# Full attention on one core: in the first head, two relu-lifted key differences per query tile and seven score banks in place of one difference and three banks

## What is computed

```python
q = (h @ wq).reshape(B, S, N_HEADS, D_HEAD)
k = (h @ wk).reshape(B, S, N_HEADS, D_HEAD)
v = (h @ wv).reshape(B, S, N_HEADS, D_HEAD)
scores = jnp.einsum('bshd,bthd->bhst', q, k) * scale
attn = jax.nn.softmax(scores, axis=-1)
ctx = jnp.einsum('bhst,bthd->bshd', attn, v).reshape(B, S, d)
X = X + ctx @ wo
```

## Time and profile before

| what | value |
|---|---|
| median of 3 runs | 2500.25 us (2498.46 to 2501.71) |
| the profiled execution: its time, its span | 2503.76 us, 2502.0 us |
| PE busy, 15464 matmuls | 2108.6 us, 84% |
| DVE busy, 4863 instructions | 1808.9 us, 72% |
| ACT busy, 2370 instructions | 1621.5 us, 65% |
| L1371 DVE maxima, 1520 | 963.6 us, mean 683 ns |
| L1368 DVE add and maximum, 264 | 182.0 us, mean 689 ns |
| L1297 ACT lifts, 264 | 157.6 us, mean 597 ns |

### The profile page before, as it was taken

The page is one execution under the profiler, slowest core; times in us unless marked ns, Lnnn a source line. Parts: engine busy times, 40 slices in busy tenths (PEclk is TensorE's granted clock), DMA queues, the critical chain, the costliest instruction groups (busy, mean ns, idle before and its releaser), DMA issues. The chain is left out here.

```text
span 2502.0 us, 44024 instructions
## 1 busy us (share of the span) xinstructions
PE 2108.6 (84%) x15464; PEld 914.0 (37%) x15464; DVE 1808.9 (72%) x4863; ACT 1621.5 (65%) x2370; POOL 516.0 (21%) x797
## 2 busy tenths in 40 slices
PE   6487488869377799999999987948999999999696
PEld 2365145657245222222222236721222222222375
DVE  7733695443585889999999925368999999996443
ACT  3033355334345479999999973424999999999443
POOL 6165131147111000000000014720000000000075
PEclk9589599879689689999999998965999999999798
DMA  2312560221480511111111021115011011010213
GB/s 67 95 44 75 76 118 16 71 57 50 85 146 16 147 25 22 24 31 23 23 30 24 8 75 32 52 38 155 16 30 30 16 30 30 16 30 2 74 47 87
DMA packets 94697, 127.17 MB, mean 51 GB/s; under 512 B 20906, under 2 KB 72592, under 8 KB 94480
## 3 DMA queue, kind: packets, MB, share of 16 engines
q1 hardware_dynamic: 82832, 102.99, 18.8%
q0 software_dynamic: 11648, 21.36, 2.9%
HBM read 79.88 MB, written 42.40 MB: 49 GB/s over the span
## 5 line engine op out<-in xcount | busy, mean ns | idle before, releaser
L1371 DVE TENSOR_REDUCE pair_mx<-ps 128x1 f32<-128x512 f32 x1520 | 963.6, 683 | 78.4 <-PE ps L1175 72.8
L1323 ACT ACTIVATE prob<-ps 128x1024 f32<-128x1024 f32 x1024 | 990.1, 1025 | 41.9 <-PE ps L1206 20.7
L1175 PE MATMUL ps<-k_stack,q_stack 48*128 48x512 bf16 x2048 | 592.9, 402 | 29.3 <-PEq L928 9.0
L1220 PE MATMUL ps<-prob,v_head 128*32 128x512 f32 x4096 | 547.7, 607 | 1.5 <-ACT prob L1323 1.0
L1206 PE MATMUL ps<-q_stack,k_stack 51*128 51x512 bf16 x2048 | 447.9, 384 | 6.0 <-ACT prob L1323 3.7
L1175 PEld LDWEIGHTS ps<-k_stack,q_stack 48*128 48x128 bf16 x2048 | 153.1, 94 | 497.5 <-DVE pair_mx L1371 354.3
L2252 DVE TENSOR_TENSOR hid<-silu,ps 128x256 f32<-128x256 f32 (+1 forms) x190 | 87.8, 463 | 246.9 <-PE ps L2105 166.2
L1206 PEld LDWEIGHTS ps<-q_stack,k_stack 51*128 51x128 bf16 x2048 | 105.1, 94 | 299.3 <-ACT prob L1323 266.8
L1722 DVE CUSTOM_DVE_ANT_0 ps<-ps,mask 128x256 f32<-128x256 f32 (+2 forms) x512 | 179.7, 418 | 40.4 <-PE ps L1526 38.2
L1297 ACT ACTIVATE qk<-ps 128x512 f32<-128x512 f32 x264 | 157.6, 597 | 62.6 <-PE ps L1175 56.0
L2105 PE MATMUL ps<-weight_raw,block 128*128 x632 | 193.9, 430 | 0.0
(11 more groups left out here) (249 smaller groups left out, 2293.1 us busy)
## 6 DMA issues: line engine op xcount, KB each, us to landing
q_stack<-image_dram SPq DMA_DIRECT2D x88, 192.0 KB, 4.6
k_stack<-k_wide_dram SPq DMA_DIRECT2D x60, 240.0 KB, 5.4
arena<-e_rows SPq DMA_DIRECT2D x32, 256.0 KB, 4.7
k_stack<-image_dram SPq DMA_DIRECT2D x32, 192.0 KB, 4.4
image_dram<-parts SPq DMA_DIRECT2D x28, 192.0 KB, 5.2
k_wide_dram<-parts SPq DMA_DIRECT2D x2, 1800.0 KB, 17.2
image_dram<-parts SPq DMA_DIRECT2D x28, 128.0 KB, 5.0
weight_raw<-in_L_ffn_Wg_dram SPq DMA_DIRECT2D x6, 528.0 KB, 4.7
```

Source lines behind the costliest of these rows:

```text
L1175: nc.tensor.matmul(max_bank(n), rows_of(c.q_stack, b, g, ROWS, slice(t * P, (t + 1) * P)), rows_of(c.k_rows, b, g, ROWS, slice(k * CHUNK, ...
L1220: ins = nc.tensor.matmul(out, c.v_head[:, e % 2, kb, :], unit, start=(kb == 0), stop=(kb == TILES - 1), skip_group_check=True)
L1323: nc.scalar.activation(c.prob[:, u % P_UNITS, :], c.ps[:, 2 * (u % 2) * CHUNK:2 * (u % 2) * CHUNK + UNIT], ACT.Exp, scale=scale).then_inc( ...
L1371: ins = nc.vector.reduce_max(mx[:, w:w + 1], max_bank(n), AX.X)
```

## The change

In head 0 the tiles 4 to 15 are now *twofold*: two products with key differences (k0 - k1, and the new k2 - k3), two lifts, and two additions with maximum. So a tile has four products, two lifts on ACT and two DVE operations. The lift buffer to add is now found by `lifts_behind`. The scores of head 0 rotate over seven banks (`FIRST_BANKS`), four of which only the exponentials of later heads use; the first two exponential units wait for their last users.

The new difference is made like the first: a second subtraction on DVE, one more unit in `UNITS`, kept where Q's columns 2048 to 2559 are free. Its three parts of head 0 are stored by `store_far` (three DMAs) and loaded by `load_far` (one per row group, two DMAs) to `k_far`, free columns behind the stacks. The rows of `k_wide_dram` become 3072 wide; `load_half` takes the first 2560. Heads 1 to 15 keep one difference.

```diff
+def load_far(engine, c, head, g, loaded):
+
+    rows = image_of(c, 1)[head * HD:(head + 1) * HD, :, FAR].rearrange("d s n -> (d s) n")
+    engine.dma_start(c.k_far[g * HALF:g * HALF + ROWS, :], rows).then_inc(loaded.sem, 16)
+
+
+def store_far(c, sp, rows, stored):
+
+    for part, where in enumerate(K_SLOTS):
+        dst = image_of(c, 1)[rows, where, FAR]
+        src = c.parts[rows, 0, part:part + 1, APART].broadcast_to((rows.stop - rows.start, dst.shape[1], CHUNK))
+        sp.dma_start(dst, src).then_inc(stored.sem, 16)
...
+FAR = slice(N_TOK + CHUNK, N_TOK + 2 * CHUNK)
...
-    return 4 if n == 0 or n == 1 and not paired else 2
+    return 6 if n == 1 and not paired else 4 if n == 0 else 2
 
 
 def first_stores(n, paired):
 
-    return 2 * PARTS if n == 1 and not paired else PARTS
+    return 3 * PARTS if n == 1 and not paired else PARTS
...
-    UNITS = [(K, k) for k in range(CHUNKS)] + [(Q, 0)] + ([] if paired else [(K, CHUNKS)]) + [(Q, k) for k in range(1, CHUNKS)]
+    NEAR, DISTANT = (K, CHUNKS), (K, CHUNKS + 1)
+    UNITS = [(K, k) for k in range(CHUNKS)] + [(Q, 0)] + ([] if paired else [NEAR, DISTANT]) + [(Q, k) for k in range(1, CHUNKS)]
...
+    def kept_at(u):
+
+        n, k = UNITS[u]
+        if UNITS[u] == DISTANT:
+            return Q, APART
+        return n, slice(k * CHUNK, (k + 1) * CHUNK)
...
-                if k == CHUNKS:
-                    pe.wait_ge(*apart.after(1))
+                if k >= CHUNKS:
+                    pe.wait_ge(*apart.after(k - CHUNKS + 1))
...
+                nc.vector.tensor_tensor(c.ht[:, FAR], c.ht[:, 2 * CHUNK:3 * CHUNK], c.ht[:, 3 * CHUNK:4 * CHUNK], ALU.subtract)\
+                    .then_inc(apart.sem, 1)
...
+                    store_far(c, sp, rows, q_stored[n])
...
+                load_far(sp, c, head, g, c.count(f"first_stack_loaded_{n}"))
...
+    FIRST_BANKS = (0, 1, 2, 3, 4, 5, 6)
...
+    def twofold(h, t):
+
+        return h == 0 and t >= FIRST_APART
...
+        if twofold(h, t):
+            return (CHUNKS, CHUNKS + 1, 1, 3)[k]
         return (CHUNKS, 2, 3, 1)[k] if apart(h, t) else k
...
+    def lifts_behind(h, w):
+
+        t, k = w // CHUNKS, w % CHUNKS
+        if twofold(h, t):
+            return (0, 0, 2, 2)[k]
+        return (0, 0, 0, 3)[k] if apart(h, t) else 0
+
     def is_lifted(key):
 
-        return key[0] not in ("turn", "rows") and keys_of(*key) == CHUNKS
+        return key[0] not in ("turn", "rows") and keys_of(*key) >= CHUNKS
...
+        return place[h, w + (2 if twofold(h, w // CHUNKS) else 3)]
...
+    def bank_of(n):
+
+        return FIRST_BANKS[n % len(FIRST_BANKS)] if n < SCORES else MAX_BANKS[n % len(MAX_BANKS)]
...
+        users = [m for m in range(max(0, n - len(FIRST_BANKS)), n) if bank_of(m) == bank_of(n)]
+        if users:
+            wait_taken(pe, users[-1])
...
+        keys = c.k_far[g * HALF:g * HALF + ROWS, :] if k > CHUNKS else rows_of(c.k_rows, b, g, ROWS, slice(k * CHUNK, (k + 1) * CHUNK))
+        nc.tensor.matmul(max_bank(n), rows_of(c.q_stack, b, g, ROWS, slice(t * P, (t + 1) * P)), keys,
+                         start=True, stop=True).then_inc(max_ready.sem, 1)
...
+            for n in range(SCORES - len(FIRST_BANKS), SCORES):
+                if bank_of(n) // 2 == u:
+                    wait_taken(pe, n)
...
-            rows = image_of(c, n)[h * HD:(h + 1) * HD].rearrange("d s n -> (d s) n")
+            rows = image_of(c, n)[h * HD:(h + 1) * HD, :, cols].rearrange("d s n -> (d s) n")
...
-                    if apart(h, w // CHUNKS) and w % CHUNKS == CHUNKS - 1:
-                        dve.wait_ge(*lifted.after(lifts_through[n]))
-                        ins = nc.vector.tensor_tensor_reduce(max_bank(n), max_bank(n), lift_buffer(lifts_through[n] - 1), 1.0, LOWEST,
+                    if lifts_behind(h, w):
+                        at = lifts_through[place[h, w - lifts_behind(h, w)]]
+                        dve.wait_ge(*lifted.after(at))
+                        ins = nc.vector.tensor_tensor_reduce(max_bank(n), max_bank(n), lift_buffer(at - 1), 1.0, LOWEST,
...
-        c.k_wide_dram = nc.dram_tensor("k_wide_dram", (D, SLOTS, N_TOK + CHUNK), bf16).ap()
+        c.k_wide_dram = nc.dram_tensor("k_wide_dram", (D, SLOTS, N_TOK + 2 * CHUNK), bf16).ap()
...
+                c.k_far = c.k_stack[:].rearrange("p b n -> p (b n)")[:, STACKS * (N_TOK + CHUNK):STACKS * (N_TOK + CHUNK) + CHUNK]
```

More of the change, by code:

```diff
@@ L950, in take_high @@
             def take_high(u):
-                n, k = UNITS[u]
+                n, cols = kept_at(u)
                 act.wait_ge(*ready.after(u + 1))
-                nc.scalar.activation(c.parts[:, n, 0, k * CHUNK:(k + 1) * CHUNK], bank(c, u % BANKS), ACT.Identity,
+                nc.scalar.activation(c.parts[:, n, 0, cols], bank(c, u % BANKS), ACT.Identity,
                                      bias=BIAS[n] if BIAS[n] is not None else 0.0).then_inc(high.sem, 1)
             def take_middle(u):
-                n, k = UNITS[u]
-                cols = slice(k * CHUNK, (k + 1) * CHUNK)
+                n, cols = kept_at(u)
                 act.wait_ge(*rest.after(u + 1))
@@ L1139, in pair_unit, with wait_taken @@
         h, w = unit_at[lift_units[i]]
-        return place[h, w + CHUNKS - 1]
+        return place[h, w + (2 if twofold(h, w // CHUNKS) else 3)]
     def lift_buffer(i):
         return c.big[:, i % LIFTS // CHUNKS, i % CHUNKS * CHUNK:(i % CHUNKS + 1) * CHUNK]
-    def wait_bank(pe, n):
[L1148 to L1155, removed]
+    def bank_of(n):
+        return FIRST_BANKS[n % len(FIRST_BANKS)] if n < SCORES else MAX_BANKS[n % len(MAX_BANKS)]
+    def wait_taken(pe, last):
+        if unit_at[last][0] == "rows":
+            pe.wait_ge(*rows_taken.after(unit_at[last][1] + 1))
+        elif is_lifted(unit_at[last]):
+            pe.wait_ge(*lifted.after(lifts_through[last]))
+        else:
+            pe.wait_ge(*max_taken.after(taken_through[last]))
+    def wait_bank(pe, n):
+        users = [m for m in range(max(0, n - len(FIRST_BANKS)), n) if bank_of(m) == bank_of(n)]
+        if users:
+            wait_taken(pe, users[-1])
     def max_bank(n):
-        return bank(c, MAX_BANKS[n % len(MAX_BANKS)])
+        return bank(c, bank_of(n))
     def rows_of(stack, b, g, n, cols):
@@ L1174, in max_unit @@
         t, k, g = w // CHUNKS, keys_of(h, w), (w + 1) % 2
-        nc.tensor.matmul(max_bank(n), rows_of(c.q_stack, b, g, ROWS, slice(t * P, (t + 1) * P)),
-                         rows_of(c.k_rows, b, g, ROWS, slice(k * CHUNK, (k + 1) * CHUNK)), start=True, stop=True).then_inc(max_ready.sem, 1)
+        keys = c.k_far[g * HALF:g * HALF + ROWS, :] if k > CHUNKS else rows_of(c.k_rows, b, g, ROWS, slice(k * CHUNK, (k + 1) * CHUNK))
+        nc.tensor.matmul(max_bank(n), rows_of(c.q_stack, b, g, ROWS, slice(t * P, (t + 1) * P)), keys,
+                         start=True, stop=True).then_inc(max_ready.sem, 1)
     def turn(pe, e):
@@ L2426, in hybrid_stack @@
         c.n = c.sbuf("n", [P, TILES, D])
-        c.ht = c.sbuf("ht", [P, N_TOK + CHUNK])
+        c.ht = c.sbuf("ht", [P, N_TOK + 2 * CHUNK])
         c.decay = c.sbuf("decay", [P, 1])
```

## The result

| | before | changed |
|---|---|---|
| median | 2499.76 us (20 runs, 2495.99 to 2502.61) | 2504.85 us (20 runs, 2499.82 to 2511.12) |
| the profiled execution: time, span | 2503.76, 2502.0 us | 2503.45, 2501.7 us |
| PE busy, matmuls | 2108.6 us, 15464 | 2083.3 us, 15468 |
| DVE busy | 1808.9 us | 1795.5 us |
| ACT busy | 1621.5 us | 1635.9 us |

What follows compares the result with a forecast made beforehand. SP's issues, the stores and the loads bound the start of head 1. Three stores (1.03) and two loads (0.92) make 1.95 us per attention, 3.9 for both, over a 2500.25 us median: 2504.2 us, range 2499 to 2509.

Steps and rivals of the forecast that it cites:

- The chain bounds, not head 0: Up to head 1's first product, SP's issues, stores and loads decide; head 0's shortening gains 0; chance 0.68 as summed.
- The rival of a shorter kernel: If head 1's load did not decide, a shorter head 0 gains 9.1 us per attention, 2482 us; chance 0.07.
- The cover named in the prediction: VectorE's work in head 0 lies beside the chain of transfers, with 2 to 3 us to spare.
- Three stores at 1.03: Stores of the new difference on SP ahead of the barrier, hidden by nothing: +1.03 us per attention.
- Two loads at 0.92: Loads of the new difference on SP ahead of the six long stores: +0.92 us per attention.
- The bytes at 0, up to 0.57: 144 KB more moved: 0 if fitting before the long stores, 0.57 us if pushing them back in full.
- Wider rows at 0: K stores and loads at pitch 6144 B for 5120: cost 0; rival, slower transfers, 2509 us, chance 0.14.
- The issues for nothing: Rival: SP's issues cost nothing because the DMA engines are behind at the long stores anyway; 2500.3 us, chance 0.07.
- Subtraction, projection unit, second lift at 0: VectorE's subtraction, the projection's extra unit, head 0's second lift: cost 0, hidden; uncovered, 0.69 (subtraction), at most 1.4 (unit).
- Head 0's length: VectorE ends head 0 at 865 to 871 us instead of 874.41; TensorE's wait before head 1 grows to 6 to 13.
- The clock: Rival: denser products in head 0 lift the clock from 1.2 to 2.4 GHz into head 1; 2498 us, chance 0.04.
- The sum against the profiled execution: 3.9 us for both attentions on the profiled 2503.76 us gives 2507.7; against the median 2500.25, 2504.2.

Runs made afterwards that it cites:

- experiment 2: Changed kernel with head 0 as before: one difference a tile, three banks, the new transfers kept but unused; 2503.37 us, ratio 1.0011.
- experiment 9: The changed kernel timed and profiled again with no edit (its second profile, "again"); 2503.85 us, ratio 1.0011 to the kernel before.
- experiment 5: Changed kernel, heads 1 and 2 stored and loaded first, the other 104 rows stored behind the first shift-row store; 2479.88 us, ratio 0.9920.
- experiment 6: The kernel before, head 0 as it was, with the cut and order of stores of experiment 5; 2494.42 us, ratio 0.9974.
- Experiment 10: Changed kernel with nine more stores of the new difference ahead of the barrier, to places nobody reads; 2509.49 us, ratio 1.0035.
- 3: Changed kernel with the three stores and two loads of the new difference issued from GpSimd instead of SP; 2502.95 us, ratio 1.0003.
- experiment 1: The kernel before with only the K rows in DRAM widened to 3072; 2500.73 us, ratio 1.0003.
- experiment 4: Changed kernel with the long stores cut in two: heads 1 and 2 stored and loaded first, then the other 104 rows; 2497.38 us, ratio 0.9989.
- 8: Changed kernel with the edits of 3 and experiment 5 together: late stores, new difference's transfers issued from GpSimd; 2479.05 us, ratio 0.9916.

## Why the prediction was right

The forecast was 2504.2 us; the medians are 2504.85 and 2503.85. The sum was 3.9 to 5.0 us; measured were 5.2 and 2.7, whose intervals both hold values from 3.7 to 4.7. That the medians lie within 0.7 us of the forecast is luck in part, with intervals more than 3 us wide; that the loss is small and comes by the chain is not. Whether the loss is over the 5.0 us named as measurable is left undecided by the two timings, as by the chances.

- *The chain bounds, not head 0*: right. Both waits for the K stack grew, and experiment 2, with head 0's old length and those waits at 3.36 and 3.86, gave the same ratio as the changed kernel in experiment 9 and the same start of head 1. The rival of a shorter kernel would have needed what experiment 5 did. The cover named in the prediction was 2 to 3 us; experiment 6 uncovered 6.6 for both attentions, as the two waits say.
- *Three stores at 1.03*: right; the block starts 1.02 and 1.03 us later. The second profile has 1.02 and, with its slow issue, 2.05. Experiment 10 gives 3.07 us for nine more.
- *Two loads at 0.92*: right in the first attention, 15.70 - 13.75 less 1.02 = 0.93. In the second a single slow issue of before blurs it (0.11; 1.15 with that issue at 0.42).
- *The bytes at 0, up to 0.57*: near 0. In the first attention the long stores took 26.80 us against 26.36, in the second 25.94 against 26.02, and again 26.65 and 26.68. The mean of the four is 26.52 against 26.19, 0.33 us more, with as much scatter between two attentions of one trace. All ten stretches with the new transfers (experiments 2, 3 and 10 too) have a mean of 26.37, the four without (before and experiment 1) 26.28; and with the nine more stores of experiment 10, 144 KB more, the long stores took 26.07 and 25.96. From the first long store to the first product of head 1 it takes 34.18 and 33.39, again 33.58 and 33.85, for the 33.6 named.
- *Wider rows at 0*: right (experiment 1). The K load's median to landing rose from 6.3 to 6.9 us in the changed kernel, but that of Q, whose pitch is the same, from 5.6 to 5.9, and from the loads' issue to the first product it took 7.25 and 7.39 us before, 7.38 and 7.45 after.
- *The issues for nothing*: fallen; both timings exclude 1, and experiment 10 doses it.
- *Subtraction, projection unit, second lift at 0*: no sign of any; experiment 2 has the first two and stays within the price of the issues, and the way to the first K store has no step. They were not run alone.
- *Head 0's length*: 25.24 us from the first maximum, within the 24.3 to 30.2 forecast (841.1 to 865.4 or 871.3). The addition's two bounds, 0.61 and 0.85, were far apart, and it measured 0.65, near the lower. So the wait came out at its upper end, 13.73 and 13.15 us, a little over the 6 to 13 named: with seven banks TensorE also ends head 0 earlier ahead of VectorE, 862.20 for 864.13, where it was 873.02 for 874.41. The absolute time, 864.13 for 865 to 871, says less: the stages ahead, with the same code, ended some 2.5 us earlier in this execution.
- *The clock*: it stayed at 0.50 through head 0 and read 0.52 in the stretch of head 1, against 0.50. No gain from it.
- *The sum against the profiled execution*, 2507.7 us: this one came to 2503.45. A single execution was not the thing to hold it to; the scatter of the twenty runs is three times the sum. The offset of 3.5 us that the prediction took off for the median was right to take off: the profiled execution of before had one of the low clocks, 0.893.

What the prediction did not see is the second transfer in line. It held that a shorter head 0 would be gained if the load of head 1 were not what decides; experiment 4 shows that TensorE then waits 10.5 and 11.9 us for the row of maxima behind the same stores.

## What to carry to other kernels

Before you shorten a stage, read what the next one waits for at its end: here 9 us per attention vanished under stores that were issued ahead of the one load needed next. Reordering those transfers brought some 25 us in the changed kernel and 6.6 in the kernel before. On the engine that came last to the barrier every DMA issue counted at its full length here, 0.33 us each, though each moved only 8 to 24 KB. When a wait is taken away, look for the next small transfer that stands in the same queue.

## What the runs showed that had not been expected

- A transfer of 12 KB issued at 865.07, behind six long stores, landed some 17 us later, and its twin on GpSimd's queue 8.5 us later (experiment 4).
- Stores of few rows move little. In the stretch of experiment 4 with the stores of 16 rows the DMA engines are as busy as ever, 0.90, at 96 GB/s, where the 120 rows had 256 to 260 at 0.83:

```profile
842.00:850.00 8.00, 7.83 (x19) 1.43 (x19) 8.00 (x18) 4.86 (x11) 0.00 (x0) 0.50 0.90 96
```

- Where GpSimd had issued three stores, the six that SP issued behind them took longer, 1.06 to 1.41 us for three in place of 0.98, in three of the four attentions of experiments 3 and 8; in the fourth, where SP's came 1.9 us and more behind GpSimd's, they took 0.98 and 1.00. Why was not tried.
